# Patch embedding channel by channel over four tiles, with its last two tiles inside layer 0's prologue

## The reference, cut to what matters

```python
patches = _patchify(x, 16)                      # x: 32 images, 3 channels, 96 x 96
tokens  = einsum('bnd,ed->bne', patches, W) + b # d = 768 = 3 channels x 256, e = 256
h = concatenate([cls_token, tokens], 1) + pos_embedding
h = concatenate([cls_tok, h], 1)                # 38 rows an image
h = h + attn(layernorm(h), Wq, Wk, Wv, Wo)      # layer 0: polynomial weights 1 + s + s*s/2, causal
h = h + linear(mxfp4(layernorm(h)), mxfp4(weight)) + bias
```

## Time and profile before

| | us |
|---|---|
| three runs | 284.48, 287.32, 288.15 |
| median | 287.32 |
| the profiled execution | 285.78 |
| its span in the profile | 284.1 |

### The profile page before, as it was taken

How to read it: one execution, slowest core, us unless ns; L and a number is a source line. 1 busy time by engine, 2 the same in 40 slices (tenths; PEclk the granted TensorE clock), 3 DMA queues, 4 the chain that set the end, 5 groups by cost and what they waited for, 6 DMA issues and landing times.

```text
span 284.1 us, 8057 instructions
## 1 busy us (share of the span) xinstructions
PE 250.1 (88%) x3292; PEld 197.7 (70%) x3292; DVE 182.9 (64%) x347; ACT 152.0 (54%) x322; POOL 157.2 (55%) x227
## 2 busy tenths in 40 slices
PE   0779989957999899897997899999999997988983
PEld 0667878845888688686886788888888884434331
DVE  0534628511559999999998588988777785534111
ACT  1312102056898868776765166675657653833450
POOL 7441324544374988787889556868676661145000
PEclk9999999999999999999999689999999999999999
DMA  5899430000000000000000000000000000002021
GB/s 176 202 248 310 106 98 0 3 0 0 3 2 2 0 2 2 2 2 3 3 2 0 2 2 2 3 3 2 3 2 5 2 3 2 0 0 68 0 66 44
DMA packets 9897, 9.81 MB, mean 35 GB/s; under 512 B 4303, under 2 KB 9030, under 8 KB 9862
## 3 DMA queue, kind: packets, MB, share of 16 engines
q1 hardware_dynamic: 9446, 9.31, 12.1%
q10 hardware_dynamic: 416, 0.01, 0.1%
HBM read 8.07 MB, written 1.25 MB: 33 GB/s over the span
## 4 chain that ended last, share of the span: by engine, by line
PE 58%; DVE 26%; issue 6%; ACT 5%; DMA 2%; POOL 2%; ACTq 0%; DVEq 0%; POOLq 0%
PE psum L1262 11%; PE psum L1298 7%; PE psum L1462 5%; PE psum L1445 5%; DVE img L1025 4%; DVE big L1018 4%; PE psum L1545 4%; PE psum L1520 3%; PE psum L1608 3%; PE psum L1596 3%; PE psum L1234 3%; DVE st L979 2%; PE psum L1535 2%; DMA w_raw<-in_L_tok_W 2%; DVE xq L1066 2%
## 5 line engine op out<-in xcount | busy, mean ns | idle before, releaser
L1298 PE MATMUL psum<-hnT,a 128*128 128x114 f32 x352 | 49.2, 284 | 1.6 <-ACT mT L695 1.2
L1298 PEld LDWEIGHTS psum<-hnT,a 128*128 128x128 f32 x352 | 44.0, 195 | 5.8 <-issue 2.1
L464 POOL TENSOR_SCALAR ve<-mvs 114x1 f32<-114x1 f32 x44 | 18.6, 422 | 52.1 <-DVE mvs L981 50.7
L1262 PE MATMUL psum<-wT,patchT 128*114 128x256 f32 x132 | 33.0, 405 | 1.6 <-DVE patchT L935 0.8
L459 POOL TENSOR_SCALAR big<-mT,parmask 128x228 f32<-128x228 f32 x22 | 22.8, 1047 | 20.9 <-ACT mT L665 20.9
L465 POOL TENSOR_TENSOR rstd<-ve,nhalf 114x1 f32<-114x1 f32 x44 | 27.8, 631 | 3.7
L485 POOL TENSOR_TENSOR big<-big,img 114x912 f32<-114x912 f32 x11 | 22.4, 2039 | 12.3 <-ACT big L729 12.3
L1262 PEld LDWEIGHTS psum<-wT,patchT 128*114 128x114 f32 x132 | 24.4, 191 | 7.0 <-DVE patchT L935 2.1
L1018 DVE SCALAR_TENSOR_TENSOR big<-big,img 114x912 f32<-114x912 f32 x11 | 17.5, 1590 | 14.8 <-ACT big L719 14.8
L719 ACT ACTIVATE big<-psum 114x912 f32<-114x912 f32 x22 | 19.3, 928 | 6.1 <-PE psum L1344 5.9
L979 DVE BATCH_NORM_STATS2 st<-h_all 114x6 f32<-114x256 f32 x44 | 18.8, 428 | 1.5
(11 more groups left out here) (156 smaller groups left out, 557.6 us busy)
## 6 DMA issues: line engine op xcount, KB each, us to landing
img<-in_x SPq DMA_DIRECT2D x6, 576.0 KB, 10.1
out<-h_all SPq DMA_DIRECT2D x10, 114.0 KB
w_raw<-in_L_tok_W SPq DMA_DIRECT2D x1, 768.0 KB, 5.9
a_raw<-in_L_attn_Wq SPq DMA_DIRECT2D x1, 256.0 KB, 8.5
a_raw<-in_L_attn_Wk SPq DMA_DIRECT2D x1, 256.0 KB, 8.6
a_raw<-in_L_attn_Wv SPq DMA_DIRECT2D x1, 256.0 KB, 8.7
a_raw<-in_L_attn_Wo SPq DMA_DIRECT2D x1, 256.0 KB, 11.9
qw<-in_L_ffn_weight SPq DMA_DIRECT2D x1, 256.0 KB, 12.0
```

The lines of the kernel that those rows point to most:

```text
L464: step(nc.gpsimd.tensor_scalar(ve[:, t:t + 1], mvs[:, t, 1:2], LN_EPS, None, ALU.add))
L1262: last = nc.tensor.matmul(EB[t % 2][0:T, 0:D], patchT[:, c, FIRST[t]:FIRST[t] + TI, :].rearrange("p b s -> p (b s)"), wT[:, c, :], start=( ...
L1298: return nc.tensor.matmul(bk[:, m * T:(m + 1) * T], w[:, c, m * 128:(m + 1) * 128], hnT[:, c, :], start=(c == 0), stop=(c == DC - 1))
```

## The change

It reorders the prologue and changes which PSUM banks it uses. No arithmetic of the result is changed.

- *TensorE.* `embed(t, channels)` issues the two matmuls of a tile and a channel. Four tiles are open at a time, each in a bank of its own (banks 4 to 7, `EB`), and go channel by channel as chunks arrive: tiles 0 to 3 on half 0, 5 to 8 on half 1, tile 4 alone. `keep_clock(n)` issues n transposes of the identity into bank 7, whose result nobody reads: 16 ahead of the wait for the weight and 12 behind the weight's transposes. Tiles 9 and 10 move into `layer0`: tile 9 behind tile 0's transpose and the four attention weights, tile 10 behind tile 0's V projection and the quantised weight.
- *ScalarE.* Odd chunks are copied ahead of the regrouping of channel 1. The copies of the attention weights come behind tile 0's norm and its transposed copy, those of the quantised weight behind tile 0's V copy. The K copy of tile 1 comes ahead of the add-one of tile 0. Two small loads (the token rows) are issued here.
- *VectorE.* Tiles, chunks and quantisation stand in a new order.
- *SP.* The two token rows are no longer issued here; the rest keeps its order.

```diff
-        EB = bank[4:6]
+        EB = [bank[n] for n in (4, 5, 6, 7, 4, 5, 6, 7, 4, 6, 6)]
+        EB_FREE = [0, 0, 0, 0, 1, 2, 3, 4, 5, 7, 10]
+        WIDE = 4
...
+        W_SLOT = bank[4:7]
...
-            sp.dma_start(tokb[0:T:S, :], dram["cls_tok"][0, :, :].to_broadcast([TI, D])).then_inc(ld_tok, 16)
-            sp.dma_start(tokb[1:T:S, :], dram["L0_tok_cls_token"][0, :, :].to_broadcast([TI, D])).then_inc(ld_tok, 16)
...
+            act.wait_ge(tok_zero, 1)
+            act.dma_start(tokb[0:T:S, :], dram["cls_tok"][0, :, :].to_broadcast([TI, D])).then_inc(ld_tok, 16)
+            act.dma_start(tokb[1:T:S, :], dram["L0_tok_cls_token"][0, :, :].to_broadcast([TI, D])).then_inc(ld_tok, 16)
...
                     patchT[:, c, half * HALF:(half + 1) * HALF, 2:S].rearrange("p b (g w) -> p b g w", w=G),
                     patch_slots(n), ACT.Copy).then_inc(img_act, 1)
-
-            for n in range(4):
...
+                if c == 1:
+                    by_patch(act, nc.scalar.copy, half, 1).then_inc(by_patch_act, 1)
             part = [wq3[:, n].rearrange("p c n -> p (c n)") for n in range(3)]
...
+            def take_a0(n):
+                act.wait_ge(a0_ps, n + 1)
+                nc.scalar.activation(a0[:, n, :, :], bank[n].rearrange("p (c e) -> p c e", c=DC), ACT.Copy
+                                     ).then_inc(a0_sb, 1)
+
             def layer0():
                 norm0(0)
                 take_hnT0(0)
+                for n in range(4):
+                    take_a0(n)
                 norm0(1)
                 take_k0(0)
                 take_v0(0)
+                weight_part(0)
                 take_q0(0)
                 take_hnT0(1)
                 norm0(2)
                 square(0)
+                take_k0(1)
                 add_one(0)
-                take_k0(1)
                 take_v0(1)
...
-            weight_part(0)
             layer0()
...
+            for n in range(CH):
+                take_w(n)
+            patches_of(0, 0)
             dve.wait_ge(consts, 2)
-            patches_of(0, 0)
...
-            for t in range(NT):
+            def take_tile(t):
                 dve.wait_ge(emb_ps, t + 1)
-                nc.vector.tensor_tensor(h_all[:, t, :], EB[t % 2][0:T, 0:D], posb[:, :], ALU.add
+                nc.vector.tensor_tensor(h_all[:, t, :], EB[t][0:T, 0:D], posb[:, :], ALU.add
...
-                if t in (0, 2, 4):
-                    take_chunk(KC + t)
-                if t == 1:
-                    patches_of(1, 2)
-                if t == EARLY:
-                    weight_scales()
-                if t == EARLY + 1:
-                    weight_grid()
-                if t == EARLY + 2:
-                    weight_rounding()
-                if t == EARLY + 3:
-                    weight_values()
+
+            take_tile(0)
+            take_tile(1)
+            take_chunk(KC)
+            take_tile(2)
+            take_tile(3)
+            patches_of(1, 2)
+            take_tile(4)
+            take_chunk(KC + 2)
+            take_chunk(KC + 4)
+            weight_scales()
+            weight_grid()
+            for t in range(EARLY, EARLY + WIDE):
+                take_tile(t)
+            weight_rounding()
+            weight_values()
+            for t in range(EARLY + WIDE, NT):
+                take_tile(t)
...
+            def keep_clock(n):
+
+                for _ in range(n):
+                    nc.tensor.transpose(bank[7][:, 0:128], ident[:, :], ident[:, :])
+
+            def turn_w(n):
...
-                if n >= 2:
-                    pe.wait_ge(a0_sb, n - 1)
                 for c in range(DC):
                     for e in range(DC):
-                        last = nc.tensor.transpose(bank[6 + n % 2][:, c * D + e * 128:c * D + (e + 1) * 128],
+                        last = nc.tensor.transpose(bank[n][:, c * D + e * 128:c * D + (e + 1) * 128],
...
+            def embed(t, channels):
+
+                for channel in channels:
+                    if channel == 0:
+                        ge(pe, emb_sb, EB_FREE[t])
+                    chunks = channel + 1 + (CH if t >= EARLY else 0)
+                    pe.wait_ge(img_dve, chunks)
+                    pe.wait_ge(img_act, chunks)
+                    for c in (2 * channel, 2 * channel + 1):
+                        last = nc.tensor.matmul(EB[t][0:T, 0:D],
+                                                patchT[:, c, FIRST[t]:FIRST[t] + TI, :].rearrange("p b s -> p (b s)"),
+                                                wT[:, c, :], start=(c == 0), stop=(c == KC - 1))
+                    if channel == CH - 1:
+                        last.then_inc(emb_ps, 1)
+
+            def turn_channel(half, channel):
+
+                for c in (2 * channel, 2 * channel + 1):
+                    turn_chunk(half * KC + c)
+
+            keep_clock(16)
+            pe.wait_ge(ld_w, 16)
+            for n in range(CH):
+                turn_w(n)
+            keep_clock(12)
+            turn_channel(0, 0)
+            pe.wait_ge(wt_sb, CH)
             pe.wait_ge(consts, 2)
...
+            for t in range(3):
+                embed(t, [0])
+            turn_channel(0, 1)
+            embed(3, [0])
+            for t in range(3):
+                embed(t, [1])
+            turn_channel(0, 2)
+            embed(3, [1])
+            for t in range(2):
+                embed(t, [2])
+            turn_channel(1, 0)
+            for t in range(2, 4):
+                embed(t, [2])
+            embed(4, range(CH))
+            turn_channel(1, 1)
+            for t in range(EARLY, EARLY + WIDE):
+                embed(t, [0])
+            turn_channel(1, 2)
+            for channel in (1, 2):
+                for t in range(EARLY, EARLY + WIDE):
+                    embed(t, [channel])
+
+            def turn_quantised_weights():
+
+                pe.wait_ge(emb_sb, EARLY + WIDE - 1)
+                pe.wait_ge(wq_ready, 1)
+                for c in range(DC):
+                    for e in range(DC):
+                        last = nc.tensor.transpose(YB[:, c * D + e * 128:c * D + (e + 1) * 128],
+                                                   wqs[:, e, c * 128:(c + 1) * 128], ident[:, :])
+                last.then_inc(wq_ps, 1)
...
+                if t == 0:
+                    pe.wait_ge(wq_sb, 1)
...
             def layer0():
+                pe.wait_ge(emb_sb, EARLY + 1)
                 turn0(0)
+                pe.wait_ge(ld_a0, 64)
+                for n in range(4):
+                    turn_weight(n)
+                embed(NT - 2, range(CH))
+                pe.wait_ge(a0_sb, 4)
+                pe.wait_ge(emb_sb, EARLY + WIDE)
                 k_proj0(0)
                 v_proj0(0)
+                turn_quantised_weights()
+                embed(NT - 1, range(CH))
                 q_proj0(0)
                 turn0(1)
                 scores0(0)
...
+                pe.wait_ge(emb_sb, NT)
...
-            pe.wait_ge(wq_sb, 1)
             layer0()
```

More of the change, by code:

```diff
@@ L325, in _, with load_channel @@
             rows = dram["x"].rearrange("b c (g p) w -> c b g (p w)", g=G)
[L327 to L330, removed]
+            def load_channel(half, c):
+                sp.dma_start(img[0:PP, half, c, :], rows[c, half * HALF:(half + 1) * HALF, :, :]
+                             ).then_inc(ld_img[half][c], 16)
             sp.dma_start(w_raw[:, :, :], dram["L0_tok_W"].rearrange("(c p) n -> p c n", p=128)).then_inc(ld_w, 16)
-            load_half(0)
+            for c in range(CH):
+                load_channel(0, c)
             sp.wait_ge(tok_zero, 1)
-            sp.dma_start(tokb[0:T:S, :], dram["cls_tok"][0, :, :].to_broadcast([TI, D])).then_inc(ld_tok, 16)
-            sp.dma_start(tokb[1:T:S, :], dram["L0_tok_cls_token"][0, :, :].to_broadcast([TI, D])).then_inc(ld_tok, 16)
             for i in range(TI):
@@ L342, in _ @@
                              ).then_inc(ld_tok, 16)
-            load_half(1)
+            for c in range(CH):
+                load_channel(1, c)
             for j, name in enumerate(["L0_attn_Wq", "L0_attn_Wk", "L0_attn_Wv", "L0_attn_Wo"]):
@@ L921, in to_blocks, with take_w @@
                 return a.rearrange("p (b o) -> p b o", o=1).to_broadcast([a.shape[0], a.shape[1], BLK])
-            for n in range(3):
+            def take_w(n):
                 dve.wait_ge(wt_ps, n + 1)
                 nc.vector.tensor_copy(wT[:, 2 * n:2 * n + 2, :],
-                                      bank[4 + n][:, :].rearrange("p (c e) -> p c e", c=2)).then_inc(wt_sb, 1)
+                                      W_SLOT[n][:, :].rearrange("p (c e) -> p c e", c=2)).then_inc(wt_sb, 1)
             def patches_of(half, c):
@@ L1214, in _ @@
             pe.wait_ge(consts, 1)
-            pe.wait_ge(ld_w, 16)
-            for n in range(3):
+            def keep_clock(n):
+                for _ in range(n):
+                    nc.tensor.transpose(bank[7][:, 0:128], ident[:, :], ident[:, :])
+            def turn_w(n):
```

(35 more changed lines are left out.)

5 lines of the change are left out of this document (removed).

## The result

The changed kernel takes 274.86 us (median of four runs, 272.63 to 275.88) against 285.9 for the kernel before on the same chip. The ratio is 0.9627, with a 95% interval from 0.9516 to 0.9738: about 11 us faster. (The ratio leaves out executions more than 1.5% above the fastest of their kernel and the medians do not, so the two need not divide exactly.) The forecast was 279.8 in a range of 274 to 284. The range holds the time and the direction is right; the forecast's own case, 277.5 to 281.5, does not hold it.

A forecast was written before the change was run, and what follows sets the result against it. TensorE, busy 250.1 of 284.1 us, was taken as the bound, with prologue pauses and a slow clock as losses. Gains of 5.1 and 0.9 made 6.0 us, taking 285.78 to 279.8; range 274 to 284.

The forecast's parts named there:

- the forecast's own case: Prologue: clock rises between 19 and 23 us, time 277.5 to 281.5 us; chance 0.38.
- The start: Prologue's first transposes: weight lands at 6.7, 16 identity transposes cost nothing, the 12 behind end at 12.46 and cost 1.2 us.
- a bound of 1.6 either way: Moved token rows, taken as zero: gain of 1.6 us if the image were late, loss of 1.6 if ScalarE were.
- The instant of the rise: Prologue: clock rises 6.0 us after matmuls start, at 21.3, inside channel 1's twelve transposes, which end at 22.1.
- the rest of the list, 36.56 by my sum: TensorE's work after 22.1 up to the first scores matmul, all at the fast clock: 36.56 us.
- Marker: Start of the first scores matmul: forecast at 58.7 instead of 63.80, 5.1 us earlier.
- The early rise: Rival, prologue: transposes do help, clock is fast from 12.8 us, time 276.1 (274 if already by the 16); chance 0.29.
- The page's rule: Trainium skill: high clock does not engage for transposes; by it the 28 identity transposes at the start buy nothing.
- The late rise: Rival, prologue: transposes interrupt the matmuls, the count restarts, clock rises at 29.0, 3.8 us lost, time 283.6; chance 0.22.
- the slower case: Rival, prologue: only the last run of 16 matmuls brings the rise, near 67; 16.6 us slower, 302; chance 0.05.
- Cover: Ahead of the first scores: tiles 9 and 10 and transposes hide tile 0's norm and weight copies; at most 2.6 us returns.
- The K copy: Tile 1's K copy moved ahead of the add-one: second scores 0.9 us earlier relative to the first, bounds 0 and 1.0.

The follow-up runs named there:

- second experiment: The kernel before, with the 16 identity transposes ahead of its wait for the weight and 12 behind the weight's transposes: 286.83 us, ratio 1.0034.
- first experiment: The changed kernel without any of its 28 identity transposes: 276.73 us, ratio 0.968 against the kernel before.
- experiments 1 and 3: 1 is the first experiment; 3 is the changed kernel with only the 16 identity transposes ahead of the weight: 277.1 us, ratio 0.9744.
- 8: Changed kernel with token rows on SP (274.11 us), rows late on ScalarE's queue (273.0), positions later (276.33), or positions later and 20 early identity transposes (273.95).

## Why the prediction was right, and where it was not

*Where the gain arises.* Right: ahead of the second scores, with the 214.1 us behind them unchanged. The repeating tile's 6.61 us carried the shift to the end one for one, in these two executions, which both have the fall in mid-run told of below.

*The start.* The 16 identity transposes ended at 5.9, as said. That the weight would land at 6.7 "whatever TensorE does" was wrong by 1.3 us: with the token rows back on SP it lands at 6.8. I had priced the moved rows at zero, with a bound of 1.6 either way that was worked out for other effects, so that it held the 1.3 is luck. It cost TensorE's start 1.2 us, of which the faster identity transposes gave the most back: they ended at 12.56 where I had 12.46.

*The instant of the rise.* This is the step that failed. "If the clock again needs 6.0 us from there, it rises at 21.3" took the one delay seen behind the first matmul as a property of matmuls. It rose at 11.6, in transposes. In the sum: I had the twelve transposes of channel 1 end at 22.1, they ended at 18.3, 3.8 us earlier; the rest of the list, 36.56 by my sum, took 36.3. Marker 58.7 forecast, 54.64 measured. The early rise, to which I gave 0.29 and 276.1 us, is the case that came (275.88 in its profiled execution). So the range held the time because it reached down to this rival, not because the forecast's mechanism was right. The rival's instant rested on the same 6.0 us, and it too was met by luck: the rise came 3.6 us behind the weight's first transpose in one execution and ahead of it in the other.

*The page's rule.* The trace of before had seemed to bear it out: 24 image transposes without a break and no rise. The changed kernel's runs contradict it, most plainly the second execution, where the weight's transposes ran at 0.11 us before any matmul. "TensorE: Matmul & The Clock Gate" in the Trainium skill (Part 4: PE-mode transpose) says the high level does not engage for them; here, for float32 transposes, it did, and the measurement decides. What I had in the rows was one kind of execution, and I read an absence there as a rule. That "128-wide transposes have not been tried here" was a misreading beside it: the weight's twelve in the earlier trace rows are 128 wide, and ran at 0.234 us each. Why the 4.3 us of transposes in the kernel before brought no rise in two executions stays open.

*The late rise and the slower case.* Neither came, in any profile of the new order. The runs without all of the identity transposes show a relative of them that I had not listed: a rise, then a fall in the pause ahead of the first matmuls, for 3.4 us at half speed.

*Cover.* The wait for tile 0's norm is gone, as said; the last 0.78 ahead of the scores stayed, as said. The K copy gave 1.0 for a forecast 0.9. VectorE, GpSimd and the image's second half stayed ahead: in the profiled execution VectorE waited 0.19 us for that half and TensorE not at all.

*Where the 10.0 us are.* Before, the marker lay 57.0 us behind the first weight transpose. The work between the two is about 41.7 us at fast prices (the prediction's list without its last wait, and the weight's 12 and first 24 image transposes and six matmuls), so 15.3 were slow time and pauses. After, it lies 46.6 behind, with 4.9 left over: the identity transposes about 1.3, slow time 1.9, pauses 1.6. That is 10.3 us less, of which 1.2 went to the late weight; the K copy added 0.8. The 15.3 of before are about 8.2 of slow time and 7.1 of pauses, so slow time shrank by about 6.3 us and the pauses by 5.5, of which 2.3 in the stretch up to the first scores. An early clock in the old order did not do it, as the second experiment shows, and the identity transposes are not needed for most of it: without them (first experiment) slow time is 3.2 and the pauses are 3.3. The pauses are the order's doing, since it gives TensorE matmuls from the moment two chunks are there. For the slow time the rise must come as early as it did; by 13.4 us at the latest the clock had risen in all eleven profiles of the new order. Why it rose there and not in the kernel before is not shown.

## What to carry to other kernels

Where an engine's first work is copied piecewise, open several accumulators and feed them channel by channel: the engine then need not wait for the whole input, and a faster clock is not eaten up by waits, as it was in the old list here (second experiment). Work that delays nothing (the last two tiles) belongs between the steps of the first chain that has nothing beside it, and a copy that the next step waits for ahead of one that nobody does. A single delay seen once, here the rise of a clock, bounds nothing: read a second execution before it carries a sum.

## What the runs showed of the hardware

*The clock can fall in a pause of under 1 us.* In the first experiment TensorE idled 1.65 us, transposed for 1.2 and idled 0.83; the clock fell at the end of that second pause, at 14.6, and the row of the stretch behind it reads 0.51. In the second it fell at 17.4, in the last of three pauses of 1.01, 1.16 and 0.79 us with transposes between. In the changed kernel the same 0.83 us pause, behind unbroken work from 8.01, brought no fall, nor did pauses of 0.69 and 0.84 us in its second execution.

*The printed clock of the start is not to be trusted.* Before the first recorded fall it stands at 1.00 in all kernels, while 128-wide transposes take 0.23 us. Durations show the level.

*The fall in mid-run.* The kernel before falls at 158.4 and again in its second execution; the changed one falls at 148.1 and 146.7, in about the same place of its list. The kernel with the token rows on SP did not fall there:

```profile
PEclk9999999999999999999999999999999999999998
```

It took 271.79 us in that execution. Its marker is 1.31 us ahead of the changed kernel's, its time 4.09; the rest, 2.8 us, is about what this fall costs, near the 3.4 that I had worked out. The kernel with the rows late says the same: its marker is 0.01 us from the changed kernel's, it did not fall there, and its span is 2.8 us shorter (271.3 against 274.1). Of the eleven profiles of the new order five lack the fall (experiments 1 and 3, and in 8 all but the one with the positions later), of the three of the old order none. That is why times of single executions are not compared here without their markers. How much of the spread of 3 to 4 us in each kernel's runs it makes is not shown, since only profiled executions tell where the clock fell.

*The same load lands at either of two times.* 6.7 to 6.8 us or 7.8 to 8.1 for the same 768 KB; both kernels that were profiled twice had it at the same of the two both times. It went with SP's list from 3.3 us on, but the transfers differ from 2 us on, before that list does. The mechanism stays open.
